# Two cross-attention and feed-forward layers on one core: an order of its own for each engine, and four operands that are no longer turned on TensorE

## The reference, cut to what matters

```python
x = x + L0_xattn(layernorm(x), ctx, ctx, ...)   # 16 heads of 32, l2-normed q and k, layernorm with gamma and beta
x = x + L0_ffn(layernorm(x), weight)            # Hadamard turn, 4-bit levels per row, ternary weight
x = x + L1_xattn(layernorm(x), ctx, ctx, ...)   # 16 heads of 32, scores clipped at 1e4
x = x + L1_ffn(layernorm(x), W1, b1, W2, b2)    # ternary W1 (2048x512) and W2 (512x2048), exact gelu
```

## Time and profile before

| what | value |
|---|---|
| median of 3 runs | 1884.29 us (1883.42 to 1885.39) |
| the profiled execution, its own time | 1877.33 us |
| its span, first to last instruction | 1875.5 us |
| steps 3 to 15, 13 steady steps | 178.4 to 1212.0 us, 79.5 us each |
| steps 16, 17, 18 | 1212.0 to 1290.0, to 1356.0, to 1402.3 us |
| phase B | 1414.0 us (first `up`) to the end; a full stage takes 57.0 us |

### The profile page before, as it was taken

How to read it: one execution, slowest core, us unless ns; L and a number is a source line. 1 busy time by engine, 2 the same in 40 slices (tenths; PEclk the granted TensorE clock), 3 DMA queues, 4 the chain that set the end, 5 groups by cost and what they waited for, 6 DMA issues and landing times. The chain is left out here.

```text
span 1875.5 us, 44682 instructions
## 1 busy us (share of the span) xinstructions
PE 1673.7 (89%) x18098; PEld 986.8 (53%) x18098; DVE 1225.7 (65%) x2444; ACT 1027.6 (55%) x1905; POOL 980.5 (52%) x1073
## 2 busy tenths in 40 slices
PE   5688898998989999989998999977759999999999
PEld 2445655556555565555565555554534444444444
DVE  4748778787787867878687786857854433344332
ACT  4663867758677586765758667586542222222221
POOL 1553857648576485855758567483353222322221
PEclk9789999999999999999999999988968999999999
DMA  7322231322313123031330313236320110011100
GB/s 225 93 88 59 65 111 24 111 58 66 111 24 111 33 91 111 19 110 25 106 100 24 111 24 111 62 112 206 112 68 19 45 45 12 34 45 46 45 23 23
DMA packets 132379, 136.47 MB, mean 73 GB/s; under 512 B 91464, under 2 KB 95688, under 8 KB 131152
## 3 DMA queue, kind: packets, MB, share of 16 engines
q1 hardware_dynamic: 129872, 125.23, 22.6%
q0 software_dynamic: 2304, 8.39, 1.1%
HBM read 72.77 MB, written 31.46 MB: 56 GB/s over the span
## 5 line engine op out<-in xcount | busy, mean ns | idle before, releaser
L802 POOL TENSOR_TENSOR arena<-arena 128x512 f16<-128x512 f32 x512 | 598.6, 1194 | 123.8 <-ACT arena L954 123.1
L946 ACT ACTIVATE arena<-psum 128x512 f32<-128x512 f32 x512 | 311.0, 614 | 78.2 <-PE psum L1413 68.1
L954 ACT ACTIVATE arena<-arena 128x512 f16<-128x512 f32 x512 | 330.5, 653 | 7.6 <-PE psum L1512 7.3
L1002 ACT ACTIVATE arena<-psum,arena 128x512 f32<-128x512 f32 x128 | 88.1, 688 | 352.1 <-PE psum L1530 352.1
L1332 PE MATMUL psum<-arena 128*128 128x512 f16 x672 | 259.8, 387 | 3.5 <-DVE arena L1084 1.8
L1333 PE MATMUL psum<-arena 128*128 128x512 f16 x672 | 258.4, 385 | 0.0
L1336 PE MATMUL psum<-arena 128*128 128x512 f16 x672 | 257.8, 384 | 0.0
L1510 PE MATMUL psum<-arena 128*128 128x33 f16 x2048 | 199.3, 180 | 62.2 <-POOL arena L802 57.3
L834 POOL TENSOR_TENSOR arena<-arena 128x512 f16<-128x512 f32 x64 | 77.3, 1208 | 333.9 <-DVE arena L1276 333.9
L1530 PE MATMUL psum<-arena 128*128 128x512 f16 x1024 | 243.1, 381 | 1.4 <-DVE arena L1269 1.4
L1540 PE MATMUL psum<-arena 128*128 128x512 f16 x1016 | 240.0, 379 | 0.9 <-POOL arena L834 0.9
(11 more groups left out here) (129 smaller groups left out, 3155.9 us busy)
## 6 DMA issues: line engine op xcount, KB each, us to landing
arena<-in_x SPq DMA_DIRECT2D x32, 512.0 KB, 4.7
arena<-x_scratch SPq DMA_DIRECT2D x32, 512.0 KB, 5.2
arena<-in_L_ffn_W SPq DMA_DIRECT2D x16, 1024.0 KB, 5.4
arena<-arena SPq DMA_DIRECT2D x16, 512.0 KB, 6.5
x_scratch<-arena POOLq DMA_DIRECT2D x16, 512.0 KB, 5.7
x_scratch<-arena SPq DMA_DIRECT2D x16, 512.0 KB, 3.0
out<-arena SPq DMA_DIRECT2D x14, 512.0 KB, 3.5
arena<-in_ctx SPq DMA_DIRECT2D x16, 384.0 KB, 5.2
```

Of the source, the lines that this page charges most:

```text
L802: gp.tensor_tensor(pl[l][:, h % NP, :], pf[l][:, h % NF, :], ph[l][:, h % NP, :], ALU.subtract).then_inc(p_lo[l].sem, 1)
L946: sc.activation(pf[l][:, h % NF, :], bank(u.bank), ACT.Exp, scale=SCALE / (QS * QS) if l == 0 else SCALE).then_inc(read[u.bank], 1)
L954: sc.activation(ph[l][:, h % NP, :], pf[l][:, h % NF, :], ACT.Copy).then_inc(p_hi[l].sem, 1)
```

## The change

1. `ORDERS` now holds five strings for each step, one for each of SP, POOL, ACT, DVE and PE, and `"steady"` for steps 3 to 15. Each engine merges the streams in its own order. The banks follow PE's order. Orders of the first and last steps are new too.
2. ctx arrives from the host as [384, 256] for each batch. One DMA lays it on the partitions as needed; `turn_ctx` is gone. `split_ctx` is one copy on ScalarE and one subtraction on VectorE of 128x768, SBUF to SBUF.
3. W1 and W2 arrive turned. `signs` writes straight into `w1T` and `w2T`; `turn_signs` and `copy_signs` are gone.
4. In phase B, ScalarE writes the fp16 upper half of the normalised rows and VectorE the lower half into `rows_b`, SBUF to SBUF, and one DMA transpose for each k, issued on SyncE, turns both halves (128x1024 fp16) into `xTb`. `turn_b` on TensorE is gone. For stage 0 this is a new kind of task, `split_b`, in step 18; there `norm_b` and `split_b` can now stand before the last tasks of stream `1b`.

In the steady steps PE's effective order differs little: without `turn_ctx`, heads 5 to 7 of `0b` follow `turn_x`; head 18 stands ahead of `project 0,1,1`; both late projections of k stand ahead of `turn_out`; `project 0,2,0`, `turn_ffn0` and `project 0,2,1` of `1f` stand ahead of `shift3`. On DVE `stats` of `1f` moves from behind head 16 to ahead of `bias0,0`; `norm0` to ahead of `clip1`; `norm1` and `unit1` by some tasks (norm1 to ahead of `out0`, unit1 to between the two `split_ffn`); `levels0` ahead of head 16 of `1b`. On ACT `split_qk 1,0` stands behind head 4, heads 6 to 8 ahead of `turn_x1`, `bias0,0` behind head 13. On POOL only `norm1`, `beta` and `out0` move by one to five heads. On SP the loads of `0f` (x and ctx) now stand ahead of the fetch of `1f`.

```diff
-def task_order(i):
+def task_order(i, engine):
     active = [0 <= i - n < B for n in range(len(ALL))]
     streams = [stream if x else [] for stream, x in zip(STREAMS, active)] + [PREPARE.get(i, [])]
-    order = ORDERS[i] if i in ORDERS else [n for n in ORDER if active[int(n)]]
+    order = ORDERS.get(i, ORDERS["steady"])[engine]
     return [(PART[task], task) for task in merged(streams, order)]
...
-def steps(emit):
+def steps(emit, engine):
     base, kept = [[0] * 8] * 2, {}
     for i in range(B + len(ALL) - 1):
-        tasks = task_order(i)
-        uses, counts = plan([task for _, task in tasks], base)
-        emit(tasks, i, i % 2, {**kept, **uses})
+        uses, counts = plan([task for _, task in task_order(i, "PE")], base)
+        emit(task_order(i, engine), i, i % 2, {**kept, **uses})
...
-    B + 1: [("mean_sum", 0)] + [x for n in range(5) for x in (("signs", n), ("turn_signs", n, 0), ("turn_signs", n, 1))],
-    B + 2: [x for n in range(5, 2 * WC) for x in (("signs", n), ("turn_signs", n, 0), ("turn_signs", n, 1))] + [("stats_b", k) for k in range(BT)] + [("rstd_b", 0)] + [("norm_b", k) for k in range(BT)],
+    B + 1: [("mean_sum", 0)] + [("signs", n) for n in range(5)],
+    B + 2: [("signs", n) for n in range(5, 2 * WC)] + [("stats_b", k) for k in range(BT)] + [("rstd_b", 0)] +
+           [(kind, k) for kind in ("norm_b", "split_b") for k in range(BT)],
...
+            def turn_b(s, slot, k):
+
+                sp.wait_ge(xTb_lo, s * BT + k + 1)
+                if s > 1:
+                    sp.wait_ge(h_filled, FC * (s - 1))
+                sp.dma_start_transpose(xTb[slot].rearrange("p s c n -> p (s c) n")[:, :, k * P:(k + 1) * P],
+                                       rows_b[:, k].rearrange("p s n -> p (s n)")).then_inc(xTb_turned, 16)
...
+            def upper_b(s, k):
+
+                act.wait_ge(xnb_ready, s * BT + k + 1)
+                later(act, xTb_turned, 16 * BT * s)
+                sc.activation(rows_b[:, k, 0, :], xnb[:, k, :], ACT.Copy).then_inc(xTb_hi, 1)
...
-                        hi(use["c", 0, at[0]], cols(cT[0], 0, at[0]), ctxT_hi.sem)
+                        act.wait_ge(ctx_loaded.sem, ctx_loaded.at(b))
+                        sc.activation(cT[0][:, 0], CT, ACT.Copy).then_inc(ctxT_hi.sem, 1)
...
+            def lower_b(s, k):
+
+                dve.wait_ge(xTb_hi, s * BT + k + 1)
+                v.tensor_tensor(rows_b[:, k, 1, :], xnb[:, k, :], rows_b[:, k, 0, :], ALU.subtract).then_inc(xTb_lo, 1)
...
-                        if 0 <= f - TURN_AT - 2 < BT:
-                            split_b(s + 1, 1 - slot, f - TURN_AT - 2)
+                        if 0 <= f - NORM_AT - 2 < BT:
+                            lower_b(s + 1, f - NORM_AT - 2)
...
-                    if has_next and 0 <= f - TURN_AT < BT:
-                        turn_b(s + 1, f - TURN_AT)
                     if has_next or f < FC - 1:
                         down(s, f)
                     if f + 2 < FC:
                         up(s, slot, f + 2)
                     elif has_next:
                         if f + 2 == FC:
-                            pe.wait_ge(xTb_read, s * BT + 2 * BT)
+                            pe.wait_ge(xTb_turned, 16 * BT * (s + 2))
                         up(s + 1, 1 - slot, f + 2 - FC)
```

More of the change, by code:

```diff
@@ L169, in front_0 @@
     out = [("load", 0), ("stats", 0), ("normalise", 0)]
-    out += [("turn_ctx", 0, k) for k in ks] + [("split_ctx", 0, k) for k in ks] + [("store_ctx", 0)]
+    out += [("split_ctx", 0), ("store_ctx", 0)]
     out += [("turn_x", 0, k) for k in ks] + [("split_x", 0, k) for k in ks]
@@ L223, in back @@
     return out
+ENGINES = ("SP", "POOL", "ACT", "DVE", "PE")
 POOLS = {"all": tuple(range(8))}
@@ L261, in kept_apart, with normalised_early @@
     return all(b < c or d < a for a, b, c, d in pairs) and in_order
+def normalised_early(tasks):
+    at = {task: n for n, task in enumerate(tasks)}
+    first, then = ("normalise", 1), ("round", 0, 0)
+    return first not in at or then not in at or at[first] < at[then]
 def kept_uses(uses):
-    kept = {name: use for name, use in uses.items() if name[0] in ("tw", "tt", "sg")}
+    kept = {name: use for name, use in uses.items() if name[0] in ("tw", "tt")}
     return {**kept, **{("mt_before", *name[1:]): use for name, use in uses.items() if name[0] == "mt"}}
-assert all(kept_apart([task for _, task in task_order(i)]) for i in range(B + len(ALL) - 1))
+assert all(kept_apart([task for _, task in task_order(i, "PE")]) for i in range(B + len(ALL) - 1))
+assert all(normalised_early([task for _, task in task_order(i, "ACT")]) for i in range(B + len(ALL) - 1))
 class Use:
@@ L387, in xattn_ffn @@
         NF, NP = 5, 4
-        pf = [tiles(take(NF * D), NF) for _ in range(2)]
+        pf_raw = [take(NF * D) for _ in range(2)]
+        pf = [tiles(a, NF) for a in pf_raw]
         ph_raw = [take(2 * NP * D // 2) for _ in range(2)]
@@ L683, in step @@
                     elif kind == "store_ctx":
-                        all_read(sp, [use["c", 0, k] for k in range(NT)])
+                        sp.wait_ge(ctxT_lo.sem, ctxT_lo.at(b))
                         sp.dma_start(batch(ctxd, b), tiles(cT_raw[0])).then_inc(ctx_stored.sem, 16)
@@ L701, in step @@
                         sp.dma_start(batch(x2d, b), X[1]).then_inc(x2_stored.sem, 16)
-            steps(step)
+            steps(step, "SP")
             def last_store(s, slot):
@@ L717, in _ @@
             for s in range(B // GB - 1):
+                for k in range(BT):
+                    turn_b(s + 1, 1 - s % 2, k)
                 store(s, s % 2)
@@ L821, in step @@
                         prep_b(0)
-            steps(step)
+            steps(step, "POOL")
             def bias_b(s, slot, k):
@@ L1251, in attn_out @@
                         ins.then_inc(read[u.bank], 1)
-            steps(step)
+            steps(step, "DVE")
             def add_b(s, slot):
@@ L1513, in attend @@
                 mm.then_inc(av_done[l].sem, 1)
-            for n, value in enumerate(steps(step)):
+            for n, value in enumerate(steps(step, "PE")):
                 pe.wait_ge(read[n], value)
-            def turn_b(s, k):
-                pe.wait_ge(xnb_ready, s * BT + k + 1)
-                later(pe, xTb_read, s * BT + k - 1)
-                for c in range(DC):
-                    mm = te.transpose(bank(6 + k % 2)[:, c * P:(c + 1) * P], xnb[:, k, c * P:(c + 1) * P], ident)
-                mm.then_inc(xTb_filled, 1)
             def up(s, slot, f):
@@ L1564, in last_down @@
                     mm.then_inc(y_filled, 1)
[L1566 to L1568 removed]
+            pe.wait_ge(wb_used, 2 * (2 * WC))
+            pe.wait_ge(xTb_turned, 16 * BT)
             up(0, 0, 0)
```

197 lines of the change are left out of this document (112 added, 85 removed).

## The result

The median fell from 1883.9 us to 1852.0 us (1848.9 to 1856.7, four runs of each): a ratio of 0.9836 [0.9808, 0.9863], 32 us less where 80 were predicted. The forecast was 1804, and its range ended at 1844.

The account below looks back on a forecast made before the run. TensorE was taken as the bound: always busy in phase B, idle 6.7 us per steady step. Gains of 47.5 + 5 + 9 + 6 + 12.5 = 80 us from 1884.3 gave 1804 us, own range 1780 to 1832, about 8 in 10 within 1765 to 1844.

Parts of the forecast that it names:

- sum of a steady step: Steps 3 to 15: four terms together shorten each of 13 steps by 3.65 us, 47.5 us in all.
- `shift3`, 2.0 us: Steady step: TensorE's 2.3 us wait for VectorE's clips mostly goes through the new order, 2.0 us gained.
- Heads and `turn_out`, 1.6 us: Steady step: of 2.5 us of waits for GpSimd's heads and for `turn_out`, 1.6 us gained.
- The fetch, -0.6 us: Steady step: ctx fetch for 1f, now behind two loads, makes TensorE wait 0.1 to 1.5 us; 0.6 lost.
- The transposes of ctx, 0.65 us gained: Steady step: six fp32 transposes leave TensorE, 0.65 us gained; their replacement on ScalarE and VectorE costs nothing.
- Steps 0 to 2, 5 us: First steps: transposes of three batches and some waits go, 5 us gained, between 0 and 10.
- Steps 16 to 18, 9 us: Last steps before phase B: `turn_signs` leaves TensorE and waits shrink, 9 us gained, between 3 and 18.
- Step 18 to phase B, 6 us: From last `out` to first `up`: statistics, norm and half the split move into step 18, 6 us gained.
- Phase B, 12.5 us: TensorE drops 16 transposes in each of 7 stages, 12.5 us gained if the DMA turns are on time.
- B: Rival: waits only move, a steady step gains its transposes and no more, 1843 us; chance 0.18.
- D: Rival: slower, ScalarE stands still at `split_ctx` waiting for the ctx load, 1917 us; chance 0.05.
- E: Rival: phase B's DMA turns come late, 21 us in each of 7 stages, 1964 us; chance 0.02.

Follow-up runs that it names:

- Experiment 1: Changed kernel with SP issuing the ctx fetch for 1f ahead of the loads of x and ctx in steady steps: 1847.9 us, 0.9821.
- Experiment 13: Changed kernel plus 20 unused fp32 transposes on TensorE ahead of its wait for the ctx fetch in each steady step: 1840.6 us, 0.9771.
- experiment 6: Changed kernel with the fetch ahead of the loads, and x and ctx for the next steady step loaded some 10 us earlier: 1833.4 us, 0.9779.
- experiment 12: Changed kernel with x and ctx loaded early, but ctx again turned on TensorE by six fp32 transposes, as before the change: 1831.7 us, 0.972.
- experiments 11: Changed kernel with x and ctx loaded early, VectorE's ctx subtraction cut to 128x256 of 128x768 from the fourth batch on: 1823.1 us, 0.9673.
- experiment 16: Changed kernel with x and ctx loaded early, ctx split moved to ScalarE's step start and right behind x's statistics on VectorE: 1815.1 us, 0.9638.

## Why the prediction was wrong

The sign and four of the mechanisms were right; the amount was not. What failed is the sum of a steady step, "0.65 + 2.0 + 1.6 - 0.6 = 3.65 us": in the trace it was 0.2 from step 4 on and 5.9 us for all thirteen where 47.5 stood, and by the medians no more than 1.3 a step (32 us less the 15 of all the rest, over 13). The rest of the sum, 32.5 us, failed by half: it was 0.4 in steps 0 to 2, -0.5 in steps 16 to 18, 5.0 to phase B and 10.0 in it.

- *`shift3`, 2.0 us.* Right and a little better: 2.6 to 0.3 for all `shift` waits, and GpSimd's wait ahead of `norm0` is gone.
- *Heads and `turn_out`, 1.6 us.* Right in the records (2.5 to 0.3 and 0.9 to 0.6), but not a gain of its own. Experiment 1 shows that as soon as the fetch is on time, 3.2 us of waiting for GpSimd come back. The GpSimd run had moved up relative to a TensorE that stood 2.5 us longer ahead of it. I had taken terms of different waits as if they add, while two of them end on loads issued at the same border.
- *The fetch, -0.6 us.* The place was right, the size was not. I had bounded it at 0.1 to 1.5 us; it was 2.6 (2.4 in the step shown). The landing took 5.8 us, where my upper end was 5.2. TensorE also came for it 3.5 us behind its issue (656.5 against 652.99), where before it came 5.0 behind the earlier trace rows, which I had not counted: the time at which a matmul "wants" its operand moves with everything that was gained ahead of it.
- *The clock, no term at all.* The wait comes with 1.65 us or more at 1.2 GHz behind it. Experiment 13 prices it by itself: 12 us by the ratios, 0.9 us a step, and up to the 1.7 us a step of the traces. The six stretches in the trace of before could have told me that; the five steps that hold them took 79.2 to 82.0 us, and the others 78.5 to 78.9.
- *The transposes of ctx, 0.65 us gained, "what replaces them I cost at nothing".* This failed, as far as the kernel with the early x can show it. The transposes were priced well: 0.5 us at equal clock (experiment 12 against the steps of 6 without low clock). What replaces them was not nothing. The subtraction of 128x768 stands in VectorE's queue ahead of the second half of `split_qk` and waits for a copy behind exps on ScalarE; shortening or moving it gave 0.2 and 0.6 us a step at equal clock, and 0.6 and 0.9 more by the low clock that went with it (experiments 11 and 16). All in all the removal made a step 0.4 us longer, 76.7 to 77.1, in place of 0.65 shorter. I had looked at how much idle time VectorE has in a step (18 us), not at what stands behind the operation. In the changed kernel itself no run took this term by itself.
- *`project` for a bank.* 1.4 us a step of a wait that the prediction did not have. The projections now stand earlier, as cover for `shift3` and `turn_out`, and their bank is still held by scores that an exp has yet to read. No run here took it away; it stands in experiment 16 as well, with 1.3 us, and is the largest wait left there, with the heads' 1.15.
- *Steps 0 to 2, 5 us.* 0.4, read at the first `project_turned` of step 3 (184.4 to 184.0 us). At that of step 2 it was 2.4 (116.1 to 113.7 us), and step 2 lost most of it again.
- *Steps 16 to 18, 9 us.* Nothing: -0.5. TensorE's busy time did fall, 49.88 to 45.42 and 25.63 to 22.17 us, but DVE's rose in step 18, 27.28 to 34.56, and in step 17 it is busy 57.6 of 68.0 us. I had noted DVE's 55.7 of 66.0 and still let 4 us out. With VectorE as the bound, TensorE's work there was cover for nothing. That DVE is what holds these steps is read from these shares; no run tested it.
- *Step 18 to phase B, 6 us.* 5.0, by the steps given: `out` and two subtractions took 1.9 us, the last one's two turns landed 5.4 us behind the first one's issue where I had 4.4.
- *Phase B, 12.5 us.* 10.0 (and 7 x 1.75 is 12.25). Each stage takes 55.2 to 55.4 us (one 56.0), 1.7 less, and no `up` waits for a DMA: the large operand turns were in time. But the first stage gained nothing, 57.5 against 57.6 us: TensorE comes to it from 8.2 us of idle time, at a granted clock of 0.50 up to 1407.3, and idles another 1.8 us in it (55.66 us busy).

So of the rivals B ("the waits only move", 1843) was nearest, for the reason that it gave, and 9 us too low, since the ends of the kernel gave 15 us and not 32.5. D and E did not happen, but D had its eye on the right task at the wrong price: not ScalarE standing still by many us, but one operation more between two halves of `split_qk`.

What remains open: the wait of `project` for its bank; why the old kernel has fewer low-clock stretches, with as much idle time in all (no run set the length of one wait alone); and where the 11 us lie by which the medians differ more than the two traces.

## What to carry to other kernels

Don't add up waits one by one: for each wait that an order removes, look for the next one that ends on the same event (here loads at the border of a step), and try the removal with the other already gone. Cost an operation "moved to an engine with idle time" by what is queued behind it, not by the engine's share. And where a trace shows TensorE standing at one place in each round and a lower granted clock behind it, count half of that stretch as lost; filling such a wait with idle matmuls is a quick test of that part. Before a shorter step is put down to the instruction that was moved, compare steps with the same clock.

## What the runs showed of the hardware

**VectorE beside GpSimd.** An operation with two SBUF inputs takes up to twice as long while GpSimd runs its subtractions of the heads. The ctx subtraction in the changed kernel and, with its instructions the same but beside a run of heads on GpSimd, in experiment 1:

```profile
L1184 DVE TENSOR_TENSOR arena<-arena 128x768 f16<-128x768 f32 x16 | 17.0, 1060 | 25.9 <-ACT arena L978 25.9
```

```profile
L1184 DVE TENSOR_TENSOR arena<-arena 128x768 f16<-128x768 f32 x16 | 27.6, 1726 | 35.0 <-ACT arena L978 35.0
```

Single ones take 0.96 us with GpSimd idle and 1.84 wholly beside a run of heads; experiment 6 has 1.3. The lower half of phase B (L1157) takes 0.68 in most cases, and 1.64 to 1.75 in eight of 32. The subtraction with one input in PSUM (L1151, 128x512) takes 0.69 in both cases. The operations that the change replaced were of that second kind, and what replaced them is of the first. The Trainium skill, "SBUF — State Buffer", section "Who interferes with whom", says that a VectorE instruction with two SBUF inputs contends with a GpSimd instruction that reads SBUF, and one with a single SBUF input does not; the trace agrees. It is not what failed the prediction, though: in the changed kernel GpSimd is idle at that moment in eleven of the thirteen steady steps, and the subtraction takes 0.96 us there.

**The clock falls behind one wait in one place.** 2.4 us of standing, then 3.3 us at 1.2 GHz, in nearly every step; with the same wait filled by idle transposes the clock stayed at 2.4 GHz from 147 to 1192 us. I had not expected that a kernel whose TensorE is busy 89% of its time pays 12 us for that.
